# Running the MLP of one query chunk inside the attention of the next, on one core of a Trainium2 chip

## The reference, cut to what matters

```
proj = quant4(x) @ ternary(Wqkv).T + b          # x: 4096 x 256, 16 heads of 16
q, k = rotary(q) @ U, rotary(k) @ U              # 32 wide
y    = softmax(q k^T / 4) @ v                    # 4096 x 4096 scores per head
x1   = layernorm(x + quant4(y) @ ternary(Wo).T)
h    = silu((x1 @ w1.T) * s1) * ((x1 @ w2.T) * s2)   # 256 -> 1024
h    = gelu((h @ h1.T) * t1)                         # 1024 -> 1024
h    = gelu((h @ h2.T) * t2)                         # 1024 -> 1024
out  = layernorm(x1 + (h @ w3.T) * s3)               # 1024 -> 256
```

## Time and profile before

| what | value |
|---|---|
| median of 3 executions | 2859.34 us (2858.58 to 2863.27) |
| the profiled execution's own time | 2857.96 us |
| its span, first to last instruction | 2856.3 us |
| PE busy | 2508.4 us (88%) |
| ACT busy | 2124.8 us (74%) |
| DVE busy | 610.1 us (21%) |
| mean granted TensorE clock | 0.966 of 2.4 GHz |

### The profile page before, as it was taken

The page is one execution under the profiler, slowest core; times in us unless marked ns, Lnnn a source line. Parts: engine busy times, 40 slices in busy tenths (PEclk is TensorE's granted clock), DMA queues, the critical chain, the costliest instruction groups (busy, mean ns, idle before and its releaser), DMA issues.

```text
span 2856.3 us, 40002 instructions
## 1 busy us (share of the span) xinstructions
PE 2508.4 (88%) x15895; PEld 1048.4 (37%) x15895; DVE 610.1 (21%) x1164; ACT 2124.8 (74%) x2360; POOL 311.4 (11%) x277
## 2 busy tenths in 40 slices
PE   2432999999999999999999999999995999999998
PEld 2220222222222222222222222222224888888887
DVE  7870000000000000000000000000005555655653
ACT  1222999999999999999999999999992223222232
POOL 2442888500000000000000000000000000000000
PEclk9765999999999999999999999999997999999999
DMA  1438444433333233323323333332222011001100
GB/s 60 130 119 228 103 99 104 93 64 63 64 63 67 58 63 63 71 64 63 62 58 67 64 64 63 69 66 60 59 45 48 1 23 22 22 0 22 22 8 16
DMA packets 94888, 178.42 MB, mean 62 GB/s; under 512 B 30432, under 2 KB 56064, under 8 KB 94208
## 3 DMA queue, kind: packets, MB, share of 16 engines
q1 hardware_dynamic: 90624, 153.05, 24.8%
q0 software_dynamic: 4096, 23.07, 3.0%
HBM read 150.63 MB, written 25.43 MB: 62 GB/s over the span
## 4 chain that ended last, share of the span: by engine, by line
ACT 34%; issue 32%; PE 25%; DVE 6%; DMA 2%; SPq 1%; ACTq 1%; DVEq 0%
ACT PB L270 34%; PE PS L517 16%; PE PS L502 4%; PE PS L529 2%; DVE TD L1060 1%; DMA KSL<-KSD 1%; ACTq L268 1%; PE PS L909 1%; DVE xq L1045 0%; DVE rq L1065 0%; DVE rq L1064 0%; DVE V L1048 0%; DVE khl L1068 0%; SPq L763 0%; DMA QSD<-shr 0%
## 5 line engine op out<-in xcount | busy, mean ns | idle before, releaser
L270 ACT ACTIVATE PB<-PS 128x1024 f32<-128x1024 f32 x2048 | 1877.7, 1237 | 1.4 <-PE PS L236 1.4
L245 PE MATMUL PS<-PB,V 128*17 128x512 f32 x8192 | 1079.3, 599 | 0.3 <-ACT PB L270 0.3
L236 PE MATMUL PS<-QSL,KSL 49*128 49x512 f32 x4096 | 753.6, 446 | 171.1 <-DMA KSL<-KSD 52.3
L236 PEld LDWEIGHTS PS<-QSL,KSL 49*128 49x128 f32 x4096 | 306.0, 185 | 1113.3 <-ACT PB L270 1060.9
L280 DVE STREAM_TRANSPOSE accS<-PS 128x512 f32<-128x512 f32 x32 | 22.9, 717 | 1874.5 <-PE PS L245 1874.5
L592 ACT ACTIVATE hfr<-PS,s 128x512 f32<-128x512 f32 x128 | 86.8, 689 | 300.5 <-PE PS L517 300.4
L245 PEld LDWEIGHTS PS<-PB,V 128*17 128x17 f32 x8192 | 136.0, 95 | 378.6 <-issue 364.1
L517 PE MATMUL PS<-hidden_ar,wh1r 128*128 128x512 f32 x1024 | 237.5, 391 | 0.0
L517 PE MATMUL PS<-hidden_br,wh2r 128*128 128x512 f32 x1024 | 235.3, 390 | 0.0
L517 PEld LDWEIGHTS PS<-hidden_br,wh2r 128*128 128x128 f32 x1024 | 191.7, 188 | 39.4
L517 PEld LDWEIGHTS PS<-hidden_ar,wh1r 128*128 128x128 f32 x1024 | 190.7, 188 | 40.1 <-DVE hfr L681 0.5
(11 more groups left out here) (135 smaller groups left out, 954.2 us busy)
## 6 DMA issues: line engine op xcount, KB each, us to landing
KSL<-KSD SPq DMA_DIRECT2D x256, 256.0 KB, 4.3
KSL<-KSD SPq DMA_DIRECT2D x256, 128.0 KB, 5.0
yq<-in_mlp POOLq DMA_DIRECT2D x44, 256.0 KB, 3.1
QSL<-QSD SPq DMA_DIRECT2D x64, 132.0 KB
QSD<-qhl SPq DMA_DIRECT2D x32, 256.0 KB
KSD<-khl SPq DMA_DIRECT2D x64, 128.0 KB
xg<-in_x SPq DMA_DIRECT2D x8, 512.0 KB, 5.7
QSL<-QSD SPq DMA_DIRECT2D x64, 64.0 KB
```

Source lines behind the costliest of these rows:

```text
L236: ins = pe.matmul(PS[:, 2 * (pair % SLOTS) + e, :], KSL[r, q % 2, s, k * P:(k + 1) * P], QSL[r, b % 2, s, :], start=True, stop=True, tile_ ...
L245: ins = pe.matmul(ACC[i * VW:i * VW + DK + 1, :], V17[:, HT * h + u, c, :], PB[:, (2 * unit + i // 2) % RING, (i % 2) * QW:(i % 2 + 1) * Q ...
L270: act.activation(PB[:, pair % RING, :], PS[:, slot:slot + 2, :].rearrange("p a b -> p (a b)"), ACT.Exp).then_inc(at["probs_ready"], 1)
```

## The change

Attention now runs in cycles of two units, 64 to a chunk (a period). A table `VISITS` says what piece of the MLP of an earlier chunk is done in which cycle: of the chunk before (lag 1) the transposition and projection of y in cycles 7, 10 and 11, the norm by cycle 13, x1's transposition in 14 and 15, layer 1 in cycles 16 to 31 (4 matmuls each), layer 2 in 32 to 47 and layer 3 in 49 to 62 (8 matmuls each: half an accumulation of one output block); of the chunk two before (lag 2) the last block of layer 3 in cycles 0 and 1, and layer 4 in 5, 6, 8 and 9 (16 matmuls each). All of these use bank 7 alone, so each use waits until the last one is read (`mlp_read`). After the eighth period two more follow without attention, with seven banks.

- PE (`fused_pe`): scores, visit, scores, and then the sums of both units.
- ACT (`fused_act`, `mlp_act`): Silu becomes a Tanh of half the argument; for layers 2 and 3 DVE moves each block to `Z`, and ACT does the eight Gelus together after the last block.
- DVE (`mlp_dve`): reads the bank, gates, splits; the eight splits come after the last block; the block's transposition of `ACC` stands behind them in its program where both fall in cycle 47.
- Weights: layers 1 to 3 are no longer held in SBUF. At the start ACT issues 24 DMAs that copy them inside DRAM into slices of 512 KB (`WRD`), and SP streams 20 slices per chunk into four slots. POOL loads only the 1 MB of layer 4. The weight check uses pieces of 1024.
- The choice between exact and inexact weights moves to the end: where a check fails, attention and a plain fp32 MLP are done again.

```diff
+VISITS = {0: (L3, 7, 0, 2), 1: (L3, 7, 1, 2), 5: (L4, 0, 0, 2), 6: (L4, 1, 0, 2), 7: (YT, 0, 0, 1), 8: (L4, 2, 0, 2),
+          9: (L4, 3, 0, 2), 10: (OP, 0, 0, 1), 11: (OP, 1, 0, 1), 14: (XT, 0, 0, 1), 15: (XT, 1, 0, 1)}
+VISITS.update({16 + i: (L1, i, 0, 1) for i in range(2 * HC)})
+VISITS.update({32 + i: (L2, i // 2, i % 2, 1) for i in range(2 * HC)})
+VISITS.update({49 + i: (L3, i // 2, i % 2, 1) for i in range(2 * HC - 2)})
...
+        def fused_pe(pe, at):
+            units = NB_ALL * KT
+            for pair in range(SLOTS):
+                scores_pe(pe, at, 0, pair)
+            for t in range(NQ):
+                for c in range(CYCLES):
+                    unit = (t * CYCLES + c) * 2
+                    for k in range(2):
+                        pe.wait_ge(at["probs_ready"], 2 * (unit + k) + 2)
+                        for pair in (2 * (unit + k) + 3, 2 * (unit + k) + 4):
+                            if pair < 2 * units:
+                                scores_pe(pe, at, 0, pair)
+                        if k == 0:
+                            mlp_pe(pe, t, c)
+                    if unit % KT == 0:
+                        pe.wait_ge(at["acc_saved"], unit // KT + 1)
+                    for k in range(2):
+                        sums_pe(pe, at, unit + k, unit // KT % NBLK)
...
+            elif stage in (L2, L3):
+                n = SLICE_OF[stage, i, g]
+                if part == 0:
+                    pe.wait_ge(slice_in[n % WSLOTS], 16 * (n // WSLOTS + 1))
+                for r in range(part * HC // PARTS_OF[stage], (part + 1) * HC // PARTS_OF[stage]):
+                    if i == 0:
+                        pe.wait_ge(hidden_split, split_count(stage, g) + r + 1)
+                    for k in range(2):
+                        ins = pe.matmul(bank, WRG[:, n % WSLOTS, r * P:(r + 1) * P], A[:, k, r, :], start=r + k == 0,
+                                        stop=r == HC - 1 and k == 1)
...
+        def mlp_act(act, t, c):
+            if c == NORMS_AT and t > 0:
+                act.wait_ge(norm_var, t)
...
+            if stage == L1 and i % 2 == 0:
+                act.wait_ge(mlp_full, USE[stage, i, g] + 1)
...
+                act.activation(SL[:, :], bank_of(stage, i, g), ACT.Tanh,
+                               scale=gates[:, 0, i // 2:i // 2 + 1]).then_inc(tanh_saved, 1)
+            if stage in (L2, L3) and i == HC - 1 and part == 1:
+                for o in range(HC):
+                    act.wait_ge(mlp_read, USE[stage, o, g] + 1)
+                    act.activation(Z[:, o, :], Z[:, o, :], ACT.Gelu).then_inc(gelu_saved, 1)
+
+        def fused_act(act, at):
...
+                act.activation(PB[:, pair % RING, :], PS[:, slot:slot + 2, :].rearrange("p a b -> p (a b)"),
+                               ACT.Exp).then_inc(at["probs_ready"], 1)
+
+                if pair % 4 == 1 and pair > 4:
+                    mlp_act(act, *divmod((pair - 5) // 4, CYCLES))
...
+                elif stage in (L2, L3) and last:
...
+                    v.tensor_scalar(Z[:, i, :], bank, s12[:, 2 if stage == L2 else 3, i:i + 1], None,
+                                    ALU.mult).then_inc(mlp_read, 1)
+                    if i == HC - 1:
+                        for o in range(HC):
+                            v.wait_ge(gelu_saved, HC * (2 * g + (stage == L3)) + o + 1)
+                            split_hidden(v, s, o)
...
+        def fused_dve(v, s, at):
+            for t in range(NQ):
+                for c in range(CYCLES):
+                    mlp_dve(v, s, t, c)
+                    if c % (KT // 2) == KT // 2 - 1:
+                        block_dve(v, at, (t * CYCLES + c) // (KT // 2))
...
+        def load_slice(sp, n):
+            if n >= WSLOTS:
+                sp.wait_ge(mlp_full, USE[FREED_BY[n - WSLOTS]] + 1)
+            sp.dma_start(WRG[:, n % WSLOTS, :].bitcast(F32), WRD[n % SLICES]).then_inc(slice_in[n % WSLOTS], 16)
...
-            load_weights(pool, True)
...
         @block.scalar
         def _(act):
+
+            n12, nh = 2 * DC * HID, HC * HID
+            w12d = a["mlp"][:, 0:n12].rearrange("p (w c n) -> p (w c) n", w=2, c=DC)
+            for o in range(HC):
+                act.dma_start(WRD[o // 2].rearrange("p (o k n) -> o p k n", o=2, n=P)[o % 2],
+                              w12d[:, :, o * P:(o + 1) * P]).then_inc(w_copied, 16)
+            for layer in range(2):
+                whd = a["mlp"][:, n12 + layer * nh:n12 + (layer + 1) * nh].rearrange("p (c n) -> p c n", c=HC)
+                for o in range(HC):
+                    act.dma_start(WRD[HC // 2 + layer * HC + o].rearrange("p (c n) -> p c n", n=P),
+                                  whd[:, :, o * P:(o + 1) * P]).then_inc(w_copied, 16)
```

More of the change, by code:

```diff
@@ L42, with visit @@
 YS = 2
-XB, FB = 3, 4
-WCHUNKS = (2 * DC * HID + 2 * HC * HID + HC * D) // QW
+XB = 3
+CW = 1024
+WCHUNKS = (2 * DC * HID + 2 * HC * HID + HC * D) // CW
+CYCLES = NBLK * KT // 2
+L1, L2, L3, L4, YT, OP, XT = "layer1", "layer2", "layer3", "layer4", "y_turned", "o_projected", "x1_turned"
+VISITS = {0: (L3, 7, 0, 2), 1: (L3, 7, 1, 2), 5: (L4, 0, 0, 2), 6: (L4, 1, 0, 2), 7: (YT, 0, 0, 1), 8: (L4, 2, 0, 2),
[3 more added lines that the diff above has]
+VISITS.update({49 + i: (L3, i // 2, i % 2, 1) for i in range(2 * HC - 2)})
+NORMS_AT = 13
+PERIODS = NQ + 2
+PARTS_OF = {L2: 2, L3: 2}
+SLICES = HC // 2 + 2 * HC
+COPIES = 3 * HC
+WSLOTS = 4
+def visit(t, c):
+    if c not in VISITS:
+        return None
+    stage, i, part, lag = VISITS[c]
+    return (stage, i, part, t - lag) if 0 <= t - lag < NQ else None
+USE, SLICE_OF = {}, {}
+for _t in range(PERIODS):
+    for _c in range(CYCLES):
+        _v = visit(_t, _c)
+        if _v is not None:
+            _stage, _i, _part, _g = _v
+            USE.setdefault((_stage, _i, _g), len(USE))
+            if _stage in (L1, L2, L3):
+                SLICE_OF[_stage, _i, _g] = SLICES * _g + {L1: _i // 4, L2: HC // 2 + _i, L3: HC // 2 + HC + _i}[_stage]
+FREED_BY = {_n: _k for _k, _n in SLICE_OF.items()}
 SUM_LOW, SUM_HIGH = 1e-26, 1e37
@@ L333, in attend_sp, with bank_of @@
             spill(blocks - 1)
+        tail_banks = (7, 0, 1, 2, 3, 4, 5)
+        def bank_of(stage, i, g):
+            use = USE[stage, i, g]
+            return PS[:, bank_number[use], :]
+        bank_number, ahead = {}, {}
+        for t in range(PERIODS):
+            for c in range(CYCLES):
+                v = visit(t, c)
+                if v is not None and USE[v[0], v[1], v[3]] not in bank_number:
+                    use = USE[v[0], v[1], v[3]]
+                    tail = t >= NQ
+                    bank_number[use] = tail_banks[use % len(tail_banks)] if tail else 7
+                    ahead[use] = max([k for k in bank_number if k < use and bank_number[k] == bank_number[use]], default=-1)
@@ L527, in layer4 @@
                     for i in range(TQ):
-                        for r in range(NP):
-                            ins = pe.matmul(out_bank[:, i, :], hidden[0][:, r, c, i * P:(i + 1) * P],
-                                            w3[:, c, :],
-                                            start=c + r == 0, stop=c == HC - 1 and r == NP - 1)
+                        ins = pe.matmul(out_bank[:, i, :], hidden[0][:, c, i * P:(i + 1) * P], w3[:, c, :],
+                                        start=c == 0, stop=c == HC - 1)
                 ins.then_inc(l_ready[3], 1)
@@ L970, in _ @@
             act.wait_ge(setup_done, 1)
-            attend_act(act, first, 0, NB_ALL, 0)
-            with act.If(sums_left_range(act)):
+            fused_act(act, first)
+            for t in range(NQ, PERIODS):
+                for c in range(CYCLES):
+                    mlp_act(act, t, c)
+            with act.If(redo(act)):
                 act.nop().then_inc(again["probs_ready"], 1)
```

500 lines of the change are left out of this document (346 added, 154 removed).

## The result

The changed kernel takes 2980.91 us (median of 4 executions, 2978.5 to 2983.34) against 2860.03 (4 executions): a ratio of 1.0421, 95% interval 1.0403 to 1.0439. It is slower by 121 us; slower had a chance of 0.80. The forecast was 3000, its range 2830 to 3090. The profiled execution took 2980.08 us with a span of 2977.2.

What follows compares the result with a forecast made beforehand. PE was to become attention's bound with the MLP laid into it, at 0.19 us free a unit. 2856.3 + 684 (attention) - 555 (tail) + 15 (setup) = 3000 us; range for 8 in 10, 2830 to 3090.

Steps and rivals of the forecast that it cites:

- The first step: Attention before the change: a unit takes 1.64 us of PE against 1.83 of ACT, leaving 0.19 us free.
- the forecast's 5.2, 4.3 and 4.13: Attention cycles of two units, in us: layer 2 or 3 visit 5.2, layer 1 visit 4.3, no visit 4.13.
- The extra 0.2 of a visit: PE at each MLP visit: 0.1 us for the shape change plus 0.1 for an exposed weight load.
- rival (a): Attention: PE cheaper than its starts show, no visit, grouped-sum or clock losses; 2735 us; chance 0.17 including up to 2853.
- The lower bound of 235 us for period 0: First attention period, without visits: 265 us forecast with grouped sums, bounds 235 to 265.
- the bank wait in layer 1: Layer 1 cycles: tanh and DVE's bank reading done about 4.8 us in, before PE's next visit at 5.0.
- 8.2 and 10.4 in the forecast: Cycle 48's Gelu burst: next release after exponentials at 8.2 us, ACC ready for the sums at about 10.4.
- Rival (c): Layer 1 on ACT: Tanh needs its own table load, 20.5 us a period, total 3165 us; chance 0.04.
- Two falls: PE's stands in both Gelu bursts: granted clock falls, 3.5 us of PE work lost each time.
- Copies: Setup: 24 DRAM-to-DRAM copies issued by ACT take 75 us, making ACT 40 us late; bounds 0 and 90.
- Keys: Setup: without 11 MB of weight loads beside them, first keys (34.87 us) take 25 us less.
- The tail: After attention's last exponential: chunk 7's serial MLP takes 158 us instead of 712.6, 555 less.

## Why the prediction was right

- **The bound.** The first step was that PE had some 0.19 us a unit free, read from start to start. Rows of idle time give other numbers: PE's matmuls leave 12.46 of 200 us idle, 0.11 a unit, and its weight loads, in the row below, wait 1060.9 us for ACT, 1.04 a unit.

```profile
L236 PEld LDWEIGHTS PS<-QSL,KSL 49*128 49x128 f32 x4096 | 306.0, 185 | 1113.3 <-ACT PB L270 1060.9
```

- **The cycles.** Those measured, 5.21, 4.30 and 4.12, are the forecast's 5.2, 4.3 and 4.13. The extra 0.2 of a visit, which no row held, is 0.20 by the two runs with one added matmul; rival (a), which took it as nothing, falls with them (a full period under 310 us was its own test, 330 came), and its light cycles of 3.67 fall with the run that changed the order alone. (Rival (a)'s sum starts attention at 247; its own terms, 262.4 - 25 with the copies hidden, give 237, and so 2725 instead of 2735.)
- **The order.** Grouped sums cost 0.45 us in two units by themselves. The lower bound of 235 us for period 0 can be had by putting the sums back (236.8), but the full periods then lose more than that, most of it by the bank wait in layer 1, which the forecast saw with 0.2 us to spare.
- **The bursts.** Release at 7.9 and ACC at 10.3 were 8.2 and 10.4 in the forecast (the terms for ACC, 1.0 + 8.5 + 0.72, add up to 10.2). Moving the transposition gave 9 us in attention. The Trainium skill, ScalarE: Activation LUTs, What ACT_TABLE_LOAD costs, adds 1.38 us to each switch; here the first load ends at 1405.41 and Gelu starts at 1405.42, the last Gelu ends at 1409.69 and the next load starts at 1409.71. So the trace disagrees, as the earlier trace rows did, and the sum without it was right. Rival (c) falls: in layer 1 Tanh starts behind an exponential and the next exponential 0.57 us after it, with no load.
- **The clock, where the sum was right in part by luck.** Two falls were counted with 3.5 us each; in period 3 there are three, the third after the norm's cycle 14 (0.51 from 1243 to 1250). From first scores to first scores cycles 2, 14 and 48 take 12.46, 8.89 and 13.86 us, the low clock in them, and cycles 15 and 49 are 1.0 us longer than others of their kind: 36.2 us, where the forecast had 30 for the three cycles and 7 for the clock. What of this the clock costs by itself was not separated; idle matmuls in two of the three gaps gave back 4 us a period. The forecast lacks a wait: cycle 6 takes 6.29 instead of 5.28, since DVE is still quantising y when layer 4's bank is full. A period's sum was right by 1 us because these errors of 1 us each have opposite signs.
- **Setup, the term that was mis-sized.** Copies: 40 in the forecast, 12 measured. Keys: 25 off in the forecast; the first key load still takes 12.88 us in the change, 22 off. Both mechanisms hold. The copies' rate was taken from SP's stores, which gives 50 us, and then put up to 75 for reading and writing DRAM, which no row asked for; 43 us were measured. (The prediction calls all 24 copies 512 KB; eight are 256 KB, and its 10.5 MB is right.) With 12 and 22 in place of 40 and 25 the same sum gives 2975 us of span against 2977.2. The prediction's own sign of being wrong, a start of attention before 260, came up by this term alone.
- **The tail.** 158 against 162.

Some seven eighths of the MLP were moved into attention, and 551 us left the tail; but attention grew by 682, since PE, which had little to give, paid 0.2 us at each of the 52 visits of layers 1 to 4, ACT and PE waited for each other in turns, and the three bursts of a period stopped both.

## What to carry to other kernels

The idle time that a profile's rows show is not the time that an engine can give away: here they said 0.11 and 1.04 us a unit, and 0.19 was right. Read the engine's work from start to start, at a place where it was not waiting, and add the price of changing the array's shape for each visit. Work laid into a two-engine chain costs least where the chain waits anyway, here between the two pairs of scores; here, slack was not carried from one cycle to the next, so even portions were better than large ones in every second cycle. Look also at what runs beside the first loads of a stage: 11 MB of weights, wanted only 1900 us later, held up the first keys for 28 us. Loading them later gave 19 us over the kernel before, and spreading them as well gave 29, the only gains over it in this study.

## What the runs showed of the hardware

- One full-array matmul between row-tiled and column-tiled ones costs 0.20 us more than one of the row-tiled shape with the same 512 columns (0.44 against 0.24 in a unit).
- During stands of PE of 7.2 us the granted clock fell from 1.00 to 0.5, 1.2 GHz, and stayed there for 6.8 to 10.3 us. 28 idle matmuls in each of 13 such gaps made the kernel 25 us faster. With another stand left in cycle 48 (1.64 us in period 3) the clock fell there in five of seven periods, and with one of 1.71 us at another place in three of seven, each time for 3.4 us.
- Tanh stands between exponentials without a table load; a table load of 1.28 us follows the last ACTIVATE after 0.02 us, and the next ACTIVATE starts 0.01 us after it.
- 24 copies of 256 or 512 KB inside DRAM, in 512-byte pieces, held ACT's queue for 43 us.
- Key loads on SP's queue beside 11 MB of loads from POOL's queue took 34.87 us (at the start) and 23.93 us (a quarter later); the first keys took 7.72 and 6.96 us with nothing of these beside them.
